# One VectorE product over three joined PSUM banks in place of three, in a linear-attention and mixture-of-experts layer

## The chip, the cores and the metric

The kernel runs on one core of one Trainium2 chip. The metric is the device time of one execution in microseconds (us). Before the change it is 228.59 us, the median of three runs (228.45 to 231.94).

## What is computed

One layer over T = 2048 tokens of width D = 128: linear attention with 16 heads of 8 channels, a layer norm, a mixture of eight experts of which each token uses two, and a second layer norm. The attention is the part that matters here:

```
q = elu(x @ Wq.T) + 1;  k = elu(x @ Wk.T) + 1;  v = x @ Wv.T        # 16 heads of 8
kv        = einsum('blhd,blhe->blhde', k, v)
kv_cumsum = cumsum(kv, axis=1);  k_cumsum = cumsum(k, axis=1)
out = einsum('blhd,blhde->blhe', q, kv_cumsum)
out = out / clip(einsum('blhd,blhd->blh', q, k_cumsum), 1e-06)
x = layernorm(x + out @ Wo.T)
```

After it come the router (softmax over 8 experts, the best two), the experts `gelu(x @ g0) * (x @ g1) @ w`, their weighted sum, and the second layer norm.

## The kernel before

The tokens are cut into 16 chunks of 128 (one token a partition), in four groups of GROUP = 4 chunks. For chunk n the attention goes through these pieces:

- `project` (PE, L566, matmul at L570) gives q, k and v in bank 0. ACT's `inputs` (L778) writes exp, relu and v; `features` (DVE, L983, instruction at L989) makes qk = the two feature maps. v1 holds v with a one behind each head's eight values, so a head has HE = 9 columns and the normalizer comes out as a ninth.
- `outer` (POOL, L475, instruction at L482) forms all products k times v: kv, 128 x 1152 (KV = 16 heads x 9 x 8), once phi_done says that qk is there. It also waits until the matmuls of the chunk four before have read its buffer.
- `prefix` (PE, L573) transposes q (L578) and then multiplies kv by a triangle of ones: the prefix sums within the chunk. The 1152 columns are split by heads into 432, 432 and 288, each in a bank of its own (banks 2, 3, 4, `pre_ps`), with one semaphore step (pre_done) each (L583). Each fp32 matmul shows as two records. Each of the three waits only for VectorE's use of the same bank for the chunk before (pre_used, L581).
- `attend` (DVE, L1002) multiplies each bank by q into prod as its matmul comes in (L1013, three instructions), sums prod over 8 channels into num (L1020), prepares the masked state of the next chunk (`mask_state`, L1000), adds num to what the running state gives (L1029), calls `features` for the chunk three on, takes denominator and reciprocal (L1034, L1037), and writes o (L1041).
- `state` (PE, L586) adds the chunk to the running state (L590) and multiplies the masked state by q (L594, bank 6). `turn_o` (L597, matmul at L601) and `put_out` (L603, L607 and L610) turn o and multiply it by Wo, adding x; ACT copies y out (L807).

Engines run in steps (`groups`, L330): in step m of group g, VectorE attends to chunk m - 1, and PE first does `project` for chunk m + 2, then `prefix` for chunk m - 1, `turn_o` of chunk m - 2, `state` of chunk m - 1 and `put_out` of chunk m - 2 (in steps with route 2, prefix comes first, and four transposes of z, L615, and the logits, L622, stand in between). PE can thus do the prefix of chunk n as soon as it has passed the state and the output of the step before; `turn_o` behind it waits for o of chunk n - 1.

From the second group on, four steps (route 0 to 3) also carry the norm and the routing of the group before, in small instructions that `attend` calls through `between(i)`, i = 0 to 8, after its own instructions: `between(0)`, `between(1)` and `between(2)` stand behind the three products. Route 0: negm at i = 1 (L1081), which ACT's four squares (L817) wait for, then vare at i = 4 (L1088), which POOL's power (L487) waits for, then shift at i = 8 (L1093). POOL's next `outer` stands behind that power. Route 1: nothing in `attend`; ACT normalises to zs, takes inputs, squares zs (L839) and copies zT (L844). Route 2 (`choose`): zsqe at i = 1 (L1104), POOL's second power (L491), the logit at i = 3 and the choice of the best two up to i = 8. Route 3 (`weigh_and_place`): esum and einv at i = 0, prob and gw at i = 1, ren and the copy of the ranks at i = 2 (L1145), then slots up to i = 8 (L1177). In these chains each small instruction waits through `Steps` (dve_steps) for the one before, except where `last` allows more. The last group has its routing done in part behind the last chunk.

POOL then scatters the rows of the last groups to DRAM (L500), a table of tiles is made, and 39 tiles of rows go through the experts (L724 to L753, L1279 to L1294, L537); a last stage adds, normalises and stores.

Of the kernel before, what the change touches and what calls it, by code (L numbers as in the profile page):

```python
# [13 lines left out]
P = 128  # L14
# [3 lines left out]
GROUP = 4  # L18
# [6 lines left out]
H, HD = 16, 8  # L25
HE = HD + 1
KV = H * HE * HD
HEADS = [(0, 6), (6, 12), (12, 16)]
E, K, HID = 8, 2, 256
HB = HID // P  # L30
REGION = T + P
# [43 lines left out]
def build(nc, xT, x, wqkv, wo, rw, rscale, pes, gate_w, lin_w, consts, out):  # L75
# [4 lines left out]
    with ExitStack() as ctx:  # L80
        def sb(name, shape, dt=F32):
            return ctx.enter_context(nc.sbuf_tensor(name, shape, dt))

        def bank(name, shape):
            return ctx.enter_context(nc.psum_tensor(name, shape, F32))

        def sem(name):
            return ctx.enter_context(nc.semaphore(name))
# [3 lines left out]
        def const(name):  # L92
            a, b = CONST[name]
            return C[:, a:b]
# [20 lines left out]
        kv = sb("kv", [P, GROUP, KV])  # L115
        prod = sb("prod", [P, KV])
# [75 lines left out]
        frs = sb("frs", [P, CHUNKS])  # L192
        fshift = sb("fshift", [P, CHUNKS])

        B = [bank(f"bank{i}", [P, 512]) for i in range(8)]

        qkv_ps = B[0]
        pre_ps = B[2:5]
        state_ps = B[5][:, 0:H * HE]
        turn_ps = B[1]  # L200
        qT_ps, oT_ps = B[1][:, 0:P], B[1][:, P:2 * P]
        inter_ps, rank_ps = B[6][:, 0:H * HE], B[6][:, 256:256 + 2 * GROUP * E]
        y_ps, lg_ps = B[7][:, 0:D], B[7][:, 256:256 + GROUP * E]
# [21 lines left out]
        pre_done = sem("pre_done")  # L225
        pre_used = sem("pre_used")
# [8 lines left out]
        summed = sem("summed")  # L235
# [90 lines left out]
        def exists(g, m):  # L326

            return not isinstance(g, int) or 0 <= GROUP * g + m < CHUNKS
# [20 lines left out]
        def after(eng, signal, count):  # L349

            if not (isinstance(count, int) and count <= 0):
                eng.wait_ge(signal, count)
# [112 lines left out]
        def _(pool):  # L465
# [9 lines left out]
            def outer(g, m):  # L475

                n, s = GROUP * g + m, m % GROUP
                pool.wait_ge(phi_done, n + 1)
                after(pool, pre_done, 3 * (n - GROUP + 1))
                a = v1[:, s, :].rearrange("p (h e) -> p h e", e=HE).unsqueeze(3).to_broadcast([P, H, HE, HD])  # L480
                b = qk[:, s, D:2 * D].rearrange("p (h d) -> p h d", d=HD).unsqueeze(2).to_broadcast([P, H, HE, HD])
                pool.tensor_tensor(kv[:, s, :].rearrange("p (h e d) -> p h e d", e=HE, d=HD), a, b,  # L482
                                   ALU.mult).then_inc(kv_done, 1)
# [21 lines left out]
            def step(g, m, route):  # L505
                if route == 0:
                    if g >= 2:
                        scatter(g - 2, (0,))
                    norm_pow(g - 1)
                if route == 2:  # L510
                    rms_pow(g - 1)
                if exists(g, m + 2):
                    outer(g, m + 2)
                if route == 0 and g >= 2:
                    scatter(g - 2, (1,))
                if route == 2 and g >= 2:
                    scatter(g - 2, (2, 3))
# [47 lines left out]
        def _(pe):  # L565
# [7 lines left out]
            def prefix(g, m):  # L573

                n, s = GROUP * g + m, m % GROUP
                pe.wait_ge(phi_done, n + 1)
                after(pe, oT_done, n - 1)
                pe.transpose(qT_ps, qk[:, s, 0:D], const("ident")).then_inc(qTp_done, 1)  # L578
                pe.wait_ge(kv_done, n + 1)
                for b, (h0, h1) in enumerate(HEADS):  # L580
                    after(pe, pre_used, 3 * (n - 1) + b + 1 if not isinstance(g, int) or n else 0)  # L581
                    c0, c1 = h0 * HE * HD, h1 * HE * HD
                    pe.matmul(pre_ps[b][:, 0:c1 - c0], const("tri"), kv[:, s, c0:c1], start=True, stop=True)\  # L583
                      .then_inc(pre_done, 1)

            def state(g, m):  # L586

# [73 lines left out]
            def step(g, m, route):  # L661
                if route == 2:
                    if exists(g, m - 1):
                        prefix(g, m - 1)
                    if exists(g, m + 2):
                        project(g, m + 2)
                    pe.wait_ge(qT_done, GROUP * g + m if exists(g, m - 1) else CHUNKS)
                    turn_z(g - 1)
                    if exists(g, m - 1):
                        state(g, m - 1)  # L670
                    pe.wait_ge(y_used, GROUP * g + m - 2 if exists(g, m - 3) else CHUNKS)
                    logits(g - 1)
                    if exists(g, m - 2):
                        turn_o(g, m - 2)
                        pe.wait_ge(lgs_done, g)
                        put_out(g, m - 2)
                    return
# [88 lines left out]
            for g in PE_PAIRS:  # L766
                c = slice(PAIR * g, PAIR * g + PAIR)
                pe.matmul(sum_ps[g], const("ident"), zall[:, c, :].rearrange("p c d -> p (c d)"),
                          start=True, stop=False)
# [198 lines left out]
        def _(ve):  # L968
# [11 lines left out]
            def heads(t, n=H):  # L980
                return t.rearrange("p (h e) -> p h e", e=HE)

            def features(g, m):  # L983

                n, s = GROUP * g + m, m % GROUP
                ve.wait_ge(act_in, 3 * (n + 1))
                after(ve, state_done, n - GROUP + 1)
                after(ve, kv_done, n - GROUP + 1)
                ve.scalar_tensor_tensor(out=qk[:, s, :], in0=eqk[:, m % 2, :], scalar=1.0, in1=rqk[:, m % 2, :],  # L989
                                        op0=ALU.min, op1=ALU.add).then_inc(phi_done, 1)  # L990

            def mask_state(g, m):

                n = GROUP * g + m
                if isinstance(g, int) and n < 1:
                    ve.wait_ge(state_zero, 1)
                else:
                    ve.wait_ge(state_done, n)
                after(ve, inter_done, n - 1)
                ve.tensor_tensor(state_m[:, m % 2, :], state_ps, const("block"), ALU.mult).then_inc(state_used, 1)  # L1000

            def attend(g, m, between):  # L1002


                n, s = GROUP * g + m, m % GROUP
                q = qk[:, s, 0:D].rearrange("p (h d) -> p h d", d=HD)
                for b, (h0, h1) in enumerate(HEADS):
                    ve.wait_ge(pre_done, 3 * n + b + 1)
                    if b == 0:
                        after(ve, summed, n)  # L1010
                    nh = h1 - h0
                    cols = nh * HE * HD
                    ve.tensor_tensor(  # L1013
                        prod[:, h0 * HE * HD:h1 * HE * HD].rearrange("p (h e d) -> p h e d", e=HE, d=HD),
                        pre_ps[b][:, 0:cols].rearrange("p (h e d) -> p h e d", e=HE, d=HD),
                        q[:, h0:h1, :].unsqueeze(2).to_broadcast([P, nh, HE, HD]), ALU.mult).then_inc(pre_used, 1)
                    between(b)
                ve.wait_ge(pre_used, 3 * (n + 1))
                after(ve, inter_used, n)
                ve.tensor_reduce(num[:, :], prod[:, :].rearrange("p (c d) -> p c d", d=HD), AX.X,  # L1020
                                 ALU.add).then_inc(summed, 1)
                between(3)
                if exists(g, m + 1):
                    mask_state(g, m + 1)
                between(4)
                ve.wait_ge(inter_done, n + 1)
                ve.wait_ge(summed, n + 1)
                after(ve, o_done, n)
                ve.tensor_tensor(inter_ps, inter_ps, num[:, :], ALU.add).then_inc(inter_used, 1)  # L1029
                if exists(g, m + 3):  # L1030
                    features(g, m + 3)
                between(5)
                ve.wait_ge(inter_used, n + 1)
                ve.tensor_scalar(den[:, :], heads(inter_ps)[:, :, HD], DEN_MIN, None, ALU.max).then_inc(den_done, 1)  # L1034
                between(6)
                ve.wait_ge(den_done, n + 1)
                ve.reciprocal(rden[:, :], den[:, :]).then_inc(rden_done, 1)  # L1037
                between(7)
                ve.wait_ge(rden_done, n + 1)
                after(ve, oTp_done, n - 1)  # L1040
                ve.tensor_tensor(o[:, m % 2, :].rearrange("p (h d) -> p h d", d=HD), heads(inter_ps)[:, :, 0:HD],  # L1041
                                 rden[:, :].unsqueeze(2).to_broadcast([P, H, HD]), ALU.mult).then_inc(o_done, 1)
                between(8)
# [209 lines left out]
            a, b = CONST["tile"]  # L1253
# [94 lines left out]
            for j in range(PAIR):  # L1348
                i = PAIR * V_PAIR + j
# [55 lines left out]
```

## Time and profile before

| | us |
|---|---|
| median of three runs | 228.59 (228.45 to 231.94) |
| the profiled execution | 230.38 |
| span of its profile | 228.5 |
| TensorE / VectorE busy | 158.9 / 160.9 |
| ScalarE / GpSimd busy | 101.1 / 124.3 |

All start times below are from the start of the span. The span has three parts: attention with routing to about 107 us, the scatters and the table to about 137 us, then the experts and the last norm. A row's second number is how long an instruction was busy: its records overlap the next one's, so the distance between two starts is what an instruction costs its engine. In a row with x3 it is the length of the three together.

### The profile page before, as it was taken

What the parts mean: (1) busy time and instruction counts of PE and PEld (TensorE: products, weight loads), DVE (VectorE), ACT (ScalarE), POOL (GpSimd) and SP (SyncE); (2) the same over time, 40 slices, a digit from 0 to 9 for tenths busy, and PEclk for the clock granted to TensorE, in tenths of its full rate; (3) what the DMA queues carried; (4) which work ended last, traced back from release to release, by engine and by line L of the source; (5) the groups of instructions that cost most, each with busy time, mean ns of one, the idle gap of its engine ahead of it and who ended that gap; (6) DMA issues with size and microseconds to landing.
All of it is one profiled execution on the core that took longest, in us unless ns stands there. A gap on an engine that the chain in (4) does not pass through costs nothing.

```text
span 228.5 us, 3949 instructions
## 1 busy us (share of the span) xinstructions
PE 158.9 (70%) x768; PEld 114.4 (50%) x769; DVE 160.9 (70%) x535; ACT 101.1 (44%) x359; POOL 124.3 (54%) x114
## 2 busy tenths in 40 slices
PE   2889989576785787675440006999999999971650
PEld 0446655353553545354330004878788888850430
DVE  0489999999989999999769911556655666621760
ACT  3315566472444723476540001556556666620270
POOL 5554643553348576447477750256566566661660
PEclk9999999999799977998555555899999999998575
DMA  5619600020000101010112533022323333215832
GB/s 158 211 27 313 269 17 0 0 80 11 1 23 12 58 12 35 26 71 25 67 51 73 149 94 93 14 79 81 80 82 97 83 82 92 71 46 134 269 96 65
DMA packets 19198, 18.54 MB, mean 81 GB/s; under 512 B 2944, under 2 KB 16256, under 8 KB 19056
## 3 DMA queue, kind: packets, MB, share of 16 engines
q1 hardware_dynamic: 16880, 13.69, 20.2%
q0 software_dynamic: 2304, 4.69, 6.2%
q8 instruction: 4, 0.07, 0.1%
q14 instruction: 10, 0.08, 0.1%
HBM read 10.60 MB, written 6.73 MB: 76 GB/s over the span
## 4 chain that ended last, share of the span: by engine, by line
PE 26%; issue 22%; DVE 18%; POOL 13%; DMA 8%; ACT 7%; DVEq 1%; SPq 1%; POOLq 1%; ACTq 0%
POOL zbuf L500 6%; POOL both L537 6%; DVE prod L1013 5%; PE bank L744 4%; PE bank L583 3%; DVE num L1020 3%; PE bank L570 3%; PE bank L733 3%; DMA both<-yout,zin 2%; PE bank L734 2%; PE bank L735 2%; DMA pl<-both 2%; DMA zin<-zbuf 2%; PE bank L773 2%; PE bank L752 2%
## 5 line engine op out<-in xcount | busy, mean ns | idle before, releaser
L537 POOL DMA_INDIRECT both<-yout,zin x39 | 37.3, 958 | 33.0 <-issue 16.6
L482 POOL TENSOR_TENSOR kv<-v,qk 128x1152 f32<-128x1152 f32 x16 | 34.8, 2174 | 30.6 <-DVE qk L989 30.6
L500 POOL DMA_INDIRECT zbuf<-rows,slot x32 | 32.6, 1018 | 13.7 <-issue 7.7
L583 PE MATMUL bank<-kv,C 128*128 128x432 f32 (+1 forms) x96 | 37.8, 533 | 2.5 <-DVE prod L1013 2.3
L583 PEld LDWEIGHTS bank<-kv,C 128*128 128x128 f32 x96 | 19.0, 212 | 18.8 <-issue 14.2
L1013 DVE TENSOR_TENSOR prod<-bank,qk 128x432 f32<-128x432 f32 (+1 forms) x48 | 24.8, 549 | 1.2 <-DVE slot L1177 0.5
L744 PE MATMUL bank<-w_l,actT 128*128 x156 | 24.7, 281 | 1.1 <-ACT actT L953 1.1
L724 PE MATMUL bank<-C,zin 128*128 128x128 f32 x39 | 11.4, 292 | 19.7 <-DMA zin<-zbuf 19.7
L744 PEld LDWEIGHTS bank<-w_l,actT 128*128 128x128 f32 x156 | 20.5, 190 | 8.9 <-issue 8.8
L1294 DVE COPY yout<-bank 128x128 f32<-128x128 f32 x39 | 11.4, 291 | 19.2 <-PE bank L744 19.2
L1020 DVE TENSOR_REDUCE num<-prod 128x144 f32<-128x1152 f32 x16 | 21.6, 1352 | 0.5
L948 ACT ACTIVATE gelu<-bank 128x256 f32<-128x256 f32 x39 | 14.9, 383 | 13.7 <-PE bank L735 13.7
L570 PE MATMUL bank<-w_qkv,xTs 128*128 128x384 f32 x32 | 17.1, 624 | 5.5 <-DMA xTs<-in_xT 3.5
L953 ACT COPY actT<-bank 128x256 f32<-128x256 f32 x39 | 14.5, 373 | 12.7 <-PE bank L752 12.7
L1279 DVE TENSOR_TENSOR zin_lo<-bank,zin_hi 128x128 fp32r<-128x128 f32 x39 | 11.4, 291 | 12.5 <-ACT zin_hi L943 8.6
L1287 DVE SCALAR_TENSOR_TENSOR act<-gelu,zin,bank 128x256 f32<-128x256 f32 x39 | 18.4, 472 | 2.3 <-ACT gelu L948 2.3
L733 PE MATMUL bank<-w_hi,zin_hi 128*128 x39 | 19.7, 505 | 0.0
L943 ACT CAST zin_hi<-bank 128x128 fp32r<-128x128 f32 x39 | 10.6, 271 | 20.0 <-PE bank L724 20.0
L724 PEld LDWEIGHTS bank<-C,zin 128*128 128x128 f32 x39 | 5.8, 148 | 20.5 <-DMA zin<-zbuf 20.4
L734 PE MATMUL bank<-w_lo,zin_hi 128*128 x39 | 16.0, 409 | 0.0
L735 PE MATMUL bank<-w_hi,zin_lo 128*128 x39 | 15.9, 408 | 0.0
L752 PE MATMUL bank<-C,act 128*128 128x128 f32 x78 | 15.1, 276 | 0.0
(152 smaller groups left out, 339.0 us busy)
## 6 DMA issues: line engine op xcount, KB each, us to landing
zin<-zbuf SPq DMA_DIRECT2D x39, 65.0 KB, 1.8
w_g<-in_gate_w SPq DMA_DIRECT2D x4, 512.0 KB, 5.9
pl<-both SPq DMA_DIRECT2D x8, 256.0 KB, 4.8
xTs<-in_xT SPq DMA_DIRECT2D x16, 64.0 KB, 2.2
w_l<-in_lin_w SPq DMA_DIRECT2D x1, 1024.0 KB, 9.1
zall<-zs SPq DMA_DIRECT2D x4, 256.0 KB, 2.4
out<-pl SPq DMA_DIRECT2D x8, 128.0 KB, 1.8
both<-yout,zin POOLq DMA_INDIRECT x39, 2.2
```

Of the source, the lines that this page charges most:

```text
L482: pool.tensor_tensor(kv[:, s, :].rearrange("p (h e d) -> p h e d", e=HE, d=HD), a, b, ALU.mult).then_inc(kv_done, 1)
L500: pool.indirect_dma_start(zbuf, bass.IndirectOffsetOnAxis(ap=slot_of(g)[:, c:c + 1].bitcast(U32), axis=0), rows_of(g)[:, j, r, :], None)\
L537: pool.indirect_dma_start(both, bass.IndirectOffsetOnAxis(ap=zin[:, b, D + 1:D + 2].bitcast(U32), axis=0), yout[:, b, :], None).then_inc(p ...
L570: pe.matmul(qkv_ps[:, 0:3 * D], xTs[:, m % GROUP, :], w_qkv[:, :], start=True, stop=True)\
L583: pe.matmul(pre_ps[b][:, 0:c1 - c0], const("tri"), kv[:, s, c0:c1], start=True, stop=True)\
L733: pe.matmul(g, zin_hi[:, b % 2, :], hi, start=True, stop=False)
L734: pe.matmul(g, zin_hi[:, b % 2, :], lo, start=False, stop=False)
L735: pe.matmul(g, zin_lo[:, b % 2, :], hi, start=False, stop=True).then_inc(gate_done, 1)
L744: mm = pe.matmul(yout_ps[b % 2][:, 0:D], actT[:, b % 2, h, :], w_l[:, bass.ds(e * (HB * D) + h * D, D)], start=(h == 0), stop=(h == HB - 1))
L752: mm = pe.transpose(actT_ps[b % 2][:, h * P:(h + 1) * P], act[:, b % 2, h * P:(h + 1) * P], const("ident"))
L1013: ve.tensor_tensor(prod[:, h0 * HE * HD:h1 * HE * HD].rearrange("p (h e d) -> p h e d", e=HE, d=HD), pre_ps[b][:, 0:cols].rearrange("p (h ...
L1020: ve.tensor_reduce(num[:, :], prod[:, :].rearrange("p (c d) -> p c d", d=HD), AX.X, ALU.add).then_inc(summed, 1)
```

## The change

The three banks become one PSUM tensor of 1536 columns. The 1152 prefix sums lie in it without gaps, so that the matmuls are cut at bank ends (512, 512, 128 columns) and no more between heads. PE waits once for the whole use of the chunk before and signals once after the third matmul; VectorE waits once, multiplies all 1152 columns in one instruction, and calls `between(0)`, `between(1)` and `between(2)` after it. The counts of pre_done and pre_used go by one a chunk. Banks 0, 1, 5, 6 and 7, and what the expert stage uses, stay where they were.

```diff
-HEADS = [(0, 6), (6, 12), (12, 16)]
+BANK = 512
+KV_PARTS = [(a, min(a + BANK, KV)) for a in range(0, KV, BANK)]
...
-        B = [bank(f"bank{i}", [P, 512]) for i in range(8)]
+        b01 = [bank(f"bank{i}", [P, BANK]) for i in range(2)]
+        b234 = bank("bank234", [P, 3 * BANK])
+        B = b01 + [b234[:, i * BANK:(i + 1) * BANK] for i in range(3)] + [bank(f"bank{i}", [P, BANK]) for i in range(5, 8)]
...
-        pre_ps = B[2:5]
+        pre_ps = b234[:, 0:KV]
...
-                after(pool, pre_done, 3 * (n - GROUP + 1))
+                after(pool, pre_done, n - GROUP + 1)
...
-                for b, (h0, h1) in enumerate(HEADS):
-                    after(pe, pre_used, 3 * (n - 1) + b + 1 if not isinstance(g, int) or n else 0)
-                    c0, c1 = h0 * HE * HD, h1 * HE * HD
-                    pe.matmul(pre_ps[b][:, 0:c1 - c0], const("tri"), kv[:, s, c0:c1], start=True, stop=True)\
-                      .then_inc(pre_done, 1)
+                after(pe, pre_used, n)
+                for c0, c1 in KV_PARTS:
+                    mm = pe.matmul(pre_ps[:, c0:c1], const("tri"), kv[:, s, c0:c1], start=True, stop=True)
+                mm.then_inc(pre_done, 1)
...
-                for b, (h0, h1) in enumerate(HEADS):
-                    ve.wait_ge(pre_done, 3 * n + b + 1)
-                    if b == 0:
-                        after(ve, summed, n)
-                    nh = h1 - h0
-                    cols = nh * HE * HD
-                    ve.tensor_tensor(
-                        prod[:, h0 * HE * HD:h1 * HE * HD].rearrange("p (h e d) -> p h e d", e=HE, d=HD),
-                        pre_ps[b][:, 0:cols].rearrange("p (h e d) -> p h e d", e=HE, d=HD),
-                        q[:, h0:h1, :].unsqueeze(2).to_broadcast([P, nh, HE, HD]), ALU.mult).then_inc(pre_used, 1)
+                ve.wait_ge(pre_done, n + 1)
+                after(ve, summed, n)
+                ve.tensor_tensor(
+                    prod[:, :].rearrange("p (h e d) -> p h e d", e=HE, d=HD),
+                    pre_ps.rearrange("p (h e d) -> p h e d", e=HE, d=HD),
+                    q.unsqueeze(2).to_broadcast([P, H, HE, HD]), ALU.mult).then_inc(pre_used, 1)
+                for b in range(3):
                     between(b)
-                ve.wait_ge(pre_used, 3 * (n + 1))
+                ve.wait_ge(pre_used, n + 1)
```

## Rows read from the trace of the kernel before

**Rows 1.** The page's first part: busy time by engine.
```profile
PE 158.9 (70%) x768; PEld 114.4 (50%) x769; DVE 160.9 (70%) x535; ACT 101.1 (44%) x359; POOL 124.3 (54%) x114
```

**Rows 2.** Busy time in one stretch of 20 us; PEclk is the granted clock.
```profile
40.00:60.00 20.00, 12.58 (x63) 8.61 (x63) 19.50 (x55) 8.64 (x37) 8.55 (x5) 0.98 0.09 27
```

**Rows 3.** Groups by line and form, 12 to 132 us: the products.
```profile
L1013 DVE TENSOR_TENSOR prod<-bank,qk 128x432 f32<-128x432 f32 x32 | 18.2, 600 | 0.9 <-DVE slot L1177 0.5
L1013 DVE TENSOR_TENSOR prod<-bank,qk 128x288 f32<-128x288 f32 x16 | 7.2, 447 | 0.4 <-PE bank L583 0.4
```

**Rows 4.** Timeline of VectorE, chunk 3: start us, busy us, instruction [idle before].
```profile
27.20 1.48 DVE L1013 TENSOR_TENSOR prod<-bank,qk 128x432 f32<-128x432 f32 x3
27.71 0.60 DVE L1013 TENSOR_TENSOR prod<-bank,qk 128x432 f32<-128x432 f32 x1
28.71 1.35 DVE L1020 TENSOR_REDUCE num<-prod 128x144 f32<-128x1152 f32 x1
29.98 0.30 DVE L1000 TENSOR_TENSOR state_m<-bank,C 128x144 f32<-128x144 f32 x1
```

**Rows 5.** Timeline of PE and VectorE, chunk 1 at the start.
```profile
17.57 2.10 PE L583 MATMUL bank<-kv,C 128*128 128x432 f32 x6
...
18.50 1.70 DVE L1013 TENSOR_TENSOR prod<-bank,qk 128x432 f32<-128x432 f32 x3
20.24 1.35 DVE L1020 TENSOR_REDUCE num<-prod 128x144 f32<-128x1152 f32 x1
```

**Rows 6.** Timeline of VectorE and POOL, a step with route 0 (chunk 9).
```profile
65.02 1.12 DVE L1013 TENSOR_TENSOR prod<-bank,qk 128x432 f32<-128x432 f32 x2 [0.48 <-DVE slot L1177]
66.06 0.16 DVE L1081 TENSOR_SCALAR negm<-ysum 128x4 f32<-128x4 f32 x1
...
68.52 0.17 DVE L1088 TENSOR_SCALAR vare<-ssq 128x4 f32<-128x4 f32 x1 [0.34 <-ACT junk L817]
...
69.80 2.16 POOL L482 TENSOR_TENSOR kv<-v,qk 128x1152 f32<-128x1152 f32 x1
69.89 2.10 DVE L1093 TENSOR_TENSOR shift<-negm,rstd 128x4 f32<-128x4 f32 x1
```

**Rows 7.** Timeline of VectorE, POOL and ACT, a step with route 2 (chunk 7).
```profile
47.09 2.18 POOL L482 TENSOR_TENSOR kv<-v,qk 128x1152 f32<-128x1152 f32 x1 [3.65 <-DVE qk L989]
47.63 1.11 DVE L1013 TENSOR_TENSOR prod<-bank,qk 128x432 f32<-128x432 f32 x2
48.66 0.64 DVE L1104 TENSOR_SCALAR zsqe<-zsq 128x4 f32<-128x4 f32 x1
...
49.69 1.35 DVE L1020 TENSOR_REDUCE num<-prod 128x144 f32<-128x1152 f32 x1
...
50.24 0.18 ACT L856 COPY lgs<-bank 128x32 f32<-128x32 f32 x1 [0.48 <-PE bank L622]
...
50.96 0.18 DVE L1053 TENSOR_TENSOR r_logit<-lgs,rrms 128x32 f32<-128x32 f32 x1
```

**Rows 8.** Timeline of VectorE, a step with route 3 (chunk 8).
```profile
56.16 0.61 DVE L1013 TENSOR_TENSOR prod<-bank,qk 128x432 f32<-128x432 f32 x1
...
56.69 0.18 DVE L1062 TENSOR_REDUCE r_esum<-r_elog 128x4 f32<-128x32 f32 x1
56.90 0.18 DVE L1066 RECIPROCAL r_einv<-r_esum 128x4 f32<-128x4 f32 x1
...
58.21 0.18 DVE L1062 TENSOR_REDUCE r_ren<-r_gw 128x4 f32<-128x32 f32 x1
...
58.44 1.34 DVE L1020 TENSOR_REDUCE num<-prod 128x144 f32<-128x1152 f32 x1
```

**Rows 9.** Timeline of PE: the prefix matmuls of chunks 7 and 12.
```profile
44.05 2.20 PE L583 MATMUL bank<-kv,C 128*128 128x432 f32 x6 [1.15 <-DVE prod L1013]
...
81.04 3.14 PE L583 MATMUL bank<-kv,C 128*128 128x432 f32 x6
```

**Rows 10.** Timeline of POOL: a scatter behind the attention.
```profile
119.46 0.96 POOL L500 DMA_INDIRECT zbuf<-rows,slot  x1 [0.30 <-ACT rows L864]
```

## The prediction

> **What bounds the kernel now.** I read the page first. No engine is busy all the time: VectorE has 160.9 of 228.5 us, PE 158.9 [rows 1]. So I went on to stretches. [...] Behind 107 us the change touches nothing. Then I read the timelines of all engines step by step, because "busy" deceives here: shift, an instruction on four columns, is busy for 2.10 us [rows 6]. It starts when POOL's kv has just begun and ends when kv ends (69.80 + 2.16 = 71.96). VectorE is held there, not working. So the question is, step by step, whether the bound is VectorE's own work, such a hold, or a chain through ACT.
>
> **One product for three.** The groups give 600 ns for 432 columns and 447 for 288 [rows 3]: 153 ns for 144 columns, 1.06 ns a column, and 141 ns besides. 1152 columns then take 1.22 + 0.14 = 1.36 us. The sum over 1152 columns has the same 1.35 us [rows 4]. Now num starts 28.71 - 27.20 = 1.51 us after the first product; the new one would let it start after 1.36 and 0.03 of semaphore, 1.39. The gain is 0.12 us a chunk, not twice the 0.14 us that each removed instruction has of its own, since neighbours overlap: the second product starts 0.51 after the first, whose record is 0.60 long [rows 4]. An instruction that needs nothing of the product starts 1.27 after it, as state_m does behind num (29.98 - 28.71) [rows 4].
>
> [...]
>
> **Product and matmuls no longer overlap.** VectorE must now wait for the third matmul, and PE for the whole product. Both ends: where the other engine is ready anyway the cost is 0; where it isn't, up to the length of the one not hidden, 2.1 us for the six records of PE at the full clock. I take it place by place.
> - Start. Chunk 1's matmuls end at 17.57 + 2.10 = 19.67. The three products now begin at 18.50 and num at 20.24 [rows 5]. Afterwards the product starts at 19.73 and num at 21.12: a loss of 0.88. Chunk 0 is late in the same way, but PE is the one that is waited for there, and it doesn't wait for VectorE.
> - Chunks 2 to 4. PE's prefix of the next chunk lies beside VectorE's num and what follows it. A chunk takes some 4.3 us; a serial pair of 1.39 and 2.1 leaves 0.8. I take 0 for the wait and the gain of 0.12 three times: +0.88 becomes +0.52. The lowest would be +0.3 (the late start partly absorbed), the highest +1.3.
> - Later steps with a PE wait: chunk 7's matmuls start at 44.05 when chunk 6's first product (43.4) has been read [rows 9]. They would start at 44.8, or 45.2 with what the start has lost, and end at 47.4; VectorE wants them at 47.63 + 0.4 = 48.0 [rows 7]. 0.6 us of cover remains. Queued behind them on PE are project, the transposes of z (for ACT's zT) and state; ACT is busy with squares till then. Cost 0. If the matmuls took 3.14 us as in chunk 12 [rows 9], the product would be 0.35 late.
> - POOL's wait on pre_done has the end of chunk n - 4; nothing hangs on it.
>
> **The small instructions, moved behind the product.**
> - Route 0 (chunks 5, 9, 13). negm starts 66.06 - 65.02 = 1.04 after the product [rows 6], afterwards 1.27: 0.23 later. On negm hangs a chain that VectorE waits for: ACT's squares, vare (VectorE idle 0.34 before it), POOL's power, POOL's kv, and shift, held until kv ends [rows 6]. So what the product gives is not gained, and 0.23 is lost. In chunk 5 negm is held by POOL's kv till after the product in both versions: 0 there, 0.23 in each of chunks 9 and 13.
> - Route 1 (chunks 6, 10, 14): no small instructions; gain 0.12.
> - Route 2 (chunks 7, 11, 15). zsqe is held till kv ends (47.09 + 2.18 = 49.27) and the third product, some 0.45, comes after it; num is at 49.69 [rows 7]. With all columns multiplied under kv, num can stand directly behind zsqe: 0.45 earlier than now relative to kv. But r_logit also needs lgs from ACT (50.24 + 0.18 = 50.42, against 50.96) [rows 7], and that comes through ACT from shift without a pause. So r_logit moves forward at most 0.5 against shift's own shift.
> - Route 3 (chunks 8, 12). Each step of the chain esum, einv, prob, gw, ren waits for the one before, 0.21 apart (56.90 - 56.69) [rows 8]; now two products cover two of these waits. Afterwards: 1.27 to esum, 4 x 0.21 to ren, 0.23 from ren to num (58.44 - 58.21), 2.34 in all against 58.44 - 56.16 = 2.28 [rows 8]. Loss 0.06. The lower end would be a gain of 0.14 (waits free), the upper a loss of 0.3.
>
> **The sum**, as VectorE's delay against before: +0.52 after chunk 4; +0.52 (chunk 5); +0.40 (6); at chunk 7 r_logit follows ACT, +0.52 - 0.51 = 0; +0.06 (8); +0.29 (9); in chunks 10 and 11 VectorE gains more than ACT lets through, so 0.29 - 0.5 = -0.2; -0.15 (12); +0.08 (13); -0.04 (14); -0.16 (15, where no kv stands in the way and only the product's 0.12 is gained). From there it goes one to one through the last routing and the scatters of POOL, the first of which wait for ACT's rows [rows 10], to the expert stage. The profiled execution took 230.38 us (span 228.5); it would take 230.2. It lies 1.8 above the median of 228.59, so the change is applied to that: 228.4. Two per cent, 4.6 us, is about what a measurement of this kernel can tell from no change; this is far inside.
>
> **Rivals.**
> 1. VectorE's own work is the bound everywhere (0.98 busy speaks for it, the holds against it). Then 16 x 0.12 = 1.9 us, and 3 x 0.35 more in route 2, less the 0.9 of the start: 2.1 faster, 226.5. Chance 0.18.
> 2. An instruction costs its whole fixed part, so that each removed one gives it back: 32 x 0.14 = 4.5 us, 224.1. The start distances [rows 4] speak against it. Chance 0.03.
> 3. The matmuls come onto the path. [...] Three times 1.4, with 0.2 of gain kept: +3.3 with the transposes and zT behind them partly beside it, 231.9. [...] Chance 0.18. [...]
> 4. The joined read is slower than three, or the joined tensor adds a stall; with 0.15 ns a column more it is 16 x 0.17 = 2.8 us, 231.2. No row has a read over a bank's end. Chance 0.05.
>
> My forecast has 0.56. Its own range is 227.4 to 229.6; with rivals 1 and 3 taken in, 226.4 to 231.4. Faster by over 2% (below 224.0) 0.02, slower by over 2% (above 233.2) 0.03, within 0.95.
>
> **What would show it.** L1013 with 16 instructions of 1.36 us and num 1.39 after each start in steps without routing; in route 2 zsqe held as before and num directly behind it; negm 1.27 after the product; route 3 with 2.3 from product to num; PE's matmuls 2.1 to 2.2 long and over before VectorE is through with o, in all chunks but 0 and 1. The forecast is wrong if VectorE is seen idle before L1013 in later chunks (rival 3), if the product is longer than 1.45 (rival 4), or if chunk 15's o comes more than 1 us earlier than now (rivals 1, 2).

## The result, and the profile after

The changed kernel takes 234.72 us (median of four runs, 232.63 to 235.37) against 228.84 for the kernel before: 5.9 us more, a ratio of 1.024 with an interval of 1.017 to 1.031. Beside other kernels on a second chip it was 232.82 against 228.32, ratio 1.0245 (1.019 to 1.030). The ratios leave out runs that lie far above the fastest of the same kernel (one of the second chip's six took 263.51), so they differ from the quotients of the medians, most for e12 below. The change is slower beyond doubt; whether by more than 2% the intervals leave open. I had forecast 228.4 with a range up to 231.4; the truth lies outside, on the side of my third rival. The profiled execution took 234.94 us, its span is 233.1 (before: 230.38 and 228.5).

First the busy times of the page, and the same 20 us stretch as in [rows 2] (columns: length, then busy time and count of PE, PEld, DVE, ACT, POOL, then the granted clock, DMA share, GB/s).

```profile
PE 161.1 (69%) x768; PEld 114.7 (49%) x769; DVE 158.3 (68%) x503; ACT 101.6 (44%) x359; POOL 124.5 (53%) x114
```

```profile
40.00:60.00 20.00, 13.58 (x54) 8.52 (x54) 16.74 (x42) 8.37 (x34) 7.88 (x5) 0.83 0.08 26
```

VectorE lost its 32 instructions and 2.6 us of busy time (holds by POOL's kv, such as the 2.10 us of shift in [rows 6], are counted in it), and the kernel is slower: in this stretch VectorE was busy for 19.50 us and is now for 16.74, and PE's clock went from 0.98 to 0.83. So VectorE waits, and the first suspect is PE. The product's own size is as forecast; the groups by form (12 to 132 us) show the product and the matmuls, first the matmuls of the kernel before:

```profile
L583 PE MATMUL bank<-kv,C 128*128 128x432 f32 x63 | 28.8, 583 | 2.5 <-DVE prod L1013 2.3
```

```profile
L585 PE MATMUL bank<-kv,C 128*128 128x512 f32 x63 | 34.5, 675 | 5.8 <-DVE prod L1011 5.8
L1011 DVE TENSOR_TENSOR prod<-bank,qk 128x1152 f32<-128x1152 f32 x16 | 21.7, 1354 | 4.9 <-PE bank L585 4.0 <-DVE slot L1176 0.5 <-issue 0.2
```

The product waits 4.0 us for the matmuls, 0.4 before [rows 3], and the matmuls 5.8 for the product, 2.3 before. Where, the timelines tell. PE's prefix matmuls of chunks 7, 11 and 12, the first and the third to be held against [rows 9]:

```profile
43.95 4.18 PE L585 MATMUL bank<-kv,C 128*128 128x512 f32 x6 [1.99 <-DVE prod L1011]
...
75.06 4.18 PE L585 MATMUL bank<-kv,C 128*128 128x512 f32 x6 [2.00 <-DVE prod L1011]
...
84.40 2.10 PE L585 MATMUL bank<-kv,C 128*128 128x512 f32 x6
```

Six records of chunk 7 took 2.20 us before, at a granted clock of 1.00 (44.05 to 46.25), and take 4.18 now, at 0.50 (43.95 to 48.13), twice the 2.10 of chunk 12 at the upper level (1.00, 84.40 to 86.50). Ahead of them PE idles 1.99 us where it idled 1.15. The chain of waits from the product of chunk 6 on shows what it does to the whole kernel:

```profile
42.46 1.36 DVE prod L1011
43.82 0.14 issue
43.95 4.18 PE bank L585 x6
48.13 1.28 PE bank L573 x2
49.41 0.63 PE bank L617 x4
50.04 0.02 issue
50.06 0.59 ACT zT L846
50.65 0.14 issue
50.79 1.04 PE bank L624 x8
51.83 0.02 issue
51.85 0.20 ACT lgs L858
```

From 43.95 to 51.83 PE is on the path almost alone: the slow matmuls, project (1.28 to the next start at a granted 0.50, in place of 0.65 at the upper level, 51.11 to 51.76 before), the transposes of z, then the logits. Two waits end last on VectorE, its product and, after it, r_logit (chunk 7, timeline of VectorE, POOL and ACT, against [rows 7]):

```profile
46.03 2.17 POOL L485 TENSOR_TENSOR kv<-v,qk 128x1152 f32<-128x1152 f32 x1 [3.52 <-DVE qk L991]
...
48.17 1.36 DVE L1011 TENSOR_TENSOR prod<-bank,qk 128x1152 f32<-128x1152 f32 x1 [1.51 <-PE bank L585]
49.44 0.16 DVE L1103 TENSOR_SCALAR zsqe<-zsq 128x4 f32<-128x4 f32 x1
49.56 1.35 DVE L1019 TENSOR_REDUCE num<-prod 128x144 f32<-128x1152 f32 x1
...
51.85 0.19 ACT L858 COPY lgs<-bank 128x32 f32<-128x32 f32 x1 [0.48 <-PE bank L624]
...
52.17 0.19 DVE L1052 TENSOR_TENSOR r_logit<-lgs,rrms 128x32 f32<-128x32 f32 x1 [1.26 <-ACT lgs L858]
```

The product is held for 1.51 us and r_logit for another 1.26. zsqe, busy 0.64 before while POOL's kv held it, is busy 0.16: kv is over when it comes (46.03 + 2.17 = 48.20).

The start of each first product, read off both timelines, gives the place of the loss in one table:

| chunk (route) | before | after | difference |
|---|---|---|---|
| 3 | 27.20 | 26.59 | -0.61 |
| 5 (0) | 36.24 | 35.31 | -0.93 |
| 6 (1) | 43.40 | 42.46 | -0.94 |
| 7 (2) | 47.63 | 48.17 | +0.54 |
| its r_logit | 50.96 | 52.17 | +1.21 |
| 8 (3) | 56.16 | 57.33 | +1.17 |
| 9 (0) | 65.02 | 66.45 | +1.43 |
| 10 (1) | 71.91 | 73.57 | +1.66 |
| 11 (2) | 76.14 | 79.27 | +3.13 |
| its r_logit | 79.48 | 83.09 | +3.61 |
| 13 (0) | 93.09 | 96.84 | +3.75 |
| 14 (1) | 97.86 | 101.83 | +3.97 |

From chunk 6 to the end the difference moves from -0.94 to the 4.6 us between the spans, by 5.5. Two jumps, 2.15 us at chunk 7 and 1.95 at chunk 11, are 4.1 of that; 0.8 comes in small steps between and behind them. The scatter that waits for ACT's rows [rows 10] is 3.98 later, and the last 0.6 comes behind it, for which no row here gives the cause:

```profile
123.44 0.96 POOL L503 DMA_INDIRECT zbuf<-rows,slot  x1 [0.30 <-ACT rows L866]
```

The small terms can be checked on the same timelines. Chunks 1 and 3, for [rows 5] and [rows 4]:

```profile
16.19 2.10 PE L585 MATMUL bank<-kv,C 128*128 128x512 f32 x6
...
18.33 1.36 DVE L1011 TENSOR_TENSOR prod<-bank,qk 128x1152 f32<-128x1152 f32 x1 [0.73 <-PE bank L585]
...
26.59 1.36 DVE L1011 TENSOR_TENSOR prod<-bank,qk 128x1152 f32<-128x1152 f32 x1
27.98 1.35 DVE L1019 TENSOR_REDUCE num<-prod 128x144 f32<-128x1152 f32 x1
```

Route 0, chunk 9, for [rows 6], and route 3, chunk 8, for [rows 8]:

```profile
57.33 1.35 DVE L1011 TENSOR_TENSOR prod<-bank,qk 128x1152 f32<-128x1152 f32 x1
...
59.72 1.34 DVE L1019 TENSOR_REDUCE num<-prod 128x144 f32<-128x1152 f32 x1
...
66.45 1.36 DVE L1011 TENSOR_TENSOR prod<-bank,qk 128x1152 f32<-128x1152 f32 x1 [0.47 <-DVE slot L1176]
67.72 0.16 DVE L1080 TENSOR_SCALAR negm<-ysum 128x4 f32<-128x4 f32 x1
...
70.18 0.17 DVE L1087 TENSOR_SCALAR vare<-ssq 128x4 f32<-128x4 f32 x1 [0.77 <-ACT junk L819]
```

num starts 1.39 us after the product, negm 1.27 after it, and 2.39 lie between product and num in route 3.

### The profile page after: what moved, and what is told of

Same layout as the page of the kernel before. It is cut to its first block, busy times and chain, and to the rows that moved or that the text cites. A ratio compares the mean times of both kernels' runs of the same rounds, so it can differ in the third digit from the quotient of the medians.

```text
span 233.1 us, 3875 instructions
## 1 busy us (share of the span) xinstructions
PE 161.1 (69%) x768; PEld 114.7 (49%) x769; DVE 158.3 (68%) x503; ACT 101.6 (44%) x359; POOL 124.5 (53%) x114
## 4 chain that ended last, share of the span: by engine, by line
PE 27%; issue 24%; POOL 16%; DVE 12%; DMA 11%; ACT 4%; SPq 1%; DVEq 1%; POOLq 1%; ACTq 0%
POOL zbuf L503 8%; PE bank L585 6%; POOL both L540 6%; DMA both<-yout,zin 3%; PE bank L573 3%; DMA zin<-zbuf 3%; PE bank L746 3%; DVE prod L1011 2%; PE bank L735 2%; DMA pl<-both 2%; PE bank L736 2%; DMA xTs<-in_xT 2%; PE bank L737 2%; PE bank L775 1%; DVE num L1019 1%
## 5 line engine op out<-in xcount | busy, mean ns | idle before, releaser
L585 PE MATMUL bank<-kv,C 128*128 128x512 f32 (+1 forms) x96 | 39.3, 551 | 5.8 <-DVE prod L1011 5.8
L1011 DVE TENSOR_TENSOR prod<-bank,qk 128x1152 f32<-128x1152 f32 x16 | 21.7, 1354 | 4.9 <-PE bank L585 4.0
```

Source lines behind the costliest of these rows:

```text
L585: mm = pe.matmul(pre_ps[:, c0:c1], const("tri"), kv[:, s, c0:c1], start=True, stop=True)
L1011: ve.tensor_tensor(prod[:, :].rearrange("p (h e d) -> p h e d", e=HE, d=HD), pre_ps.rearrange("p (h e d) -> p h e d", e=HE, d=HD), q.unsqu ...
```

## The experiments

Theory A: PE must wait for the whole product, idles longer before the prefix of chunks 7 and 11, and its clock falls. Theory B: what costs is that product and matmuls no longer overlap, at any clock. Times are medians. The four sets (e1 to e4; e5 to e8; e9 to e12; e13 to e16) ran each on a chip of its own, with the kernel before beside them (229.11, 228.32, 229.49 and 228.87 us); between sets the ratios are what can be compared.

**e1, PE's wait alone.**

```diff
+                after(pe, pre_used, 3 * n)
                 for b, (h0, h1) in enumerate(HEADS):
-                    after(pe, pre_used, 3 * (n - 1) + b + 1 if not isinstance(g, int) or n else 0)
```

> The kernel before, with one edit: PE waits for all three products of the chunk before ahead of its first prefix matmul, as in the change; three banks, three products and three signals stay. [...] Theory B (what costs is that product and matmuls no longer overlap, whatever the clock): at most 0.5 us slower, since the product here still begins behind the first matmul.

Measured: 233.37 against 229.11, ratio 1.012 (1.008 to 1.017). The matmuls of chunks 7 and 11:

```profile
44.12 3.81 PE L583 MATMUL bank<-kv,C 128*128 128x432 f32 x6 [2.02 <-DVE prod L1013]
...
73.64 3.19 PE L583 MATMUL bank<-kv,C 128*128 128x432 f32 x6 [2.03 <-DVE prod L1013]
```

As theory A has it, by the medians (+4.3): idle 2.0, the clock low for most of both (granted 0.57 and 0.67). By the ratio it is 2.8 us, just under the 3 to 4.5 that A expected, and about half of the change's 5.5. Theory B's 0.5 is passed either way.

**e2, VectorE's wait alone.**

```diff
-                    ve.wait_ge(pre_done, 3 * n + b + 1)
                     if b == 0:
+                        ve.wait_ge(pre_done, 3 * n + 3)
```

> The kernel before, with one edit: VectorE waits for the third matmul of the chunk ahead of its first product; PE may still refill each bank as it comes free. Theory A: PE's idle time and clock stay as before, 0 to 1 us slower (only the start of the attention pays). Theory B: nearly all of the loss of the change, 3 to 5 us slower.

Measured: 230.83, ratio 1.008 (1.004 to 1.013), 1.7 us by the medians and 1.9 by the ratio: more than A's upper end, well short of B. The start accounts for 1.1: chunk 5's first product begins at 36.52, against 35.46 in e4, which differs from the kernel before only behind chunk 5, both with first matmuls of 3.5 us. And one of its two matmul groups was slow (3.67 us, granted clock 0.59), though PE idled only 1.14:

```profile
44.32 3.67 PE L583 MATMUL bank<-kv,C 128*128 128x432 f32 x6 [1.14 <-DVE prod L1013]
...
73.02 2.20 PE L583 MATMUL bank<-kv,C 128*128 128x432 f32 x6 [1.16 <-DVE prod L1013]
```

**e3, the changed kernel with PE kept busy; e4, the kernel before with the same.** In route 2 steps, before the wait for the product; in route 1 the state's own matmul leaves its signal to the last of the six.

```diff
                 pe.transpose(qT_ps, qk[:, s, 0:D], const("ident")).then_inc(qTp_done, 1)
+                for _ in range(warm):
+                    mm = pe.matmul(state_ps, zero[:, 0:P], zero[:, :], start=False, stop=False,
+                                   skip_group_check=True)
+                if warm:
+                    mm.then_inc(state_done, 1)
...
```

> The changed kernel, with six small matmuls of zeros times zeros added to the running state (they add nothing) ahead of the prefix matmuls of chunks 7, 11 and 15, where PE waits for the whole product. [...] Theory B: no faster than the changed kernel, 234 or more, since PE has more to do and overlaps as little.

> The kernel before with the same six small matmuls at the same place, as a control. Theory A: the clock was full there already, so within 1 us of before, up to 0.5 us slower where they hold back the prefix. If instead it gets faster by 2 us or more, the small matmuls help somewhere else, and the gain of the run with the changed kernel says less about chunks 7 and 11.

Measured: e3 228.94, ratio to before 1.000 (0.997 to 1.003), so the whole loss of the change is gone (theory A expected 229 to 231); e4 229.82, ratio 1.003 (1.000 to 1.006), the control. In e3:

```profile
41.98 1.64 PE L584 MATMUL bank<-zero 128*128 128x144 f32 x12
44.13 2.18 PE L591 MATMUL bank<-kv,C 128*128 128x512 f32 x6 [0.52 <-DVE prod L1019]
...
73.14 2.18 PE L591 MATMUL bank<-kv,C 128*128 128x512 f32 x6 [0.53 <-DVE prod L1019]
```

Both groups ran at a granted clock of 1.00. Product and matmuls overlap as little as in the changed kernel, and more work made it some 4 to 6 us faster. Theory B falls as the main cause; what is left of it is the start and the 1.9 us at most that e2 shows.

**e8, the changed kernel once more; e5, with negm ahead of the product.**

```diff
+                first()
                 ve.wait_ge(pre_done, n + 1)
...
-                    if route is not None:
+                    if route is not None and (route, i) != (0, 1):
...
-                    attend(g, m - 1, between)
+                    attend(g, m - 1, between, (lambda: parts[0](g - 1, 1)) if route == 0 else (lambda: None))
```

> The changed kernel as it is, beside the others on the same chip: both theories expect 233 to 235.5, 4 to 6 us over the kernel before, with the prefix matmuls of chunks 7 and 11 at about 4.2 us.

> The changed kernel with negm (route 0) ahead of the product in place of behind it. My step on route 0 says that negm starts the chain that VectorE waits for (squares, vare, power, kv, shift), and that the change put it from 1.04 to 1.27 us behind the product's start. If that is right: negm comes 1.2 to 1.3 us earlier, VectorE's idle time before vare (0.62 to 0.81 us three times) goes, and the time falls by 1.5 to 2.5 us against the changed kernel run beside it; the prefix matmuls of chunks 7 and 11 stay at 4.2 us. If route 0 is not a bound, no change.

Measured: e8 232.82, with 3.68 and 3.78 us for the matmuls of chunks 7 and 11; e5 230.71 (ratio 1.010, 1.006 to 1.014), so 2.1 us for moving one instruction on four columns. Chunk 9 in e5: negm stands before the product, and vare has no idle time before it (0.77 in the changed kernel).

```profile
66.64 0.17 DVE L1081 TENSOR_SCALAR negm<-ysum 128x4 f32<-128x4 f32 x1 [0.38 <-DVE slot L1177]
66.86 1.36 DVE L1012 TENSOR_TENSOR prod<-bank,qk 128x1152 f32<-128x1152 f32 x1
...
69.73 0.16 DVE L1088 TENSOR_SCALAR vare<-ssq 128x4 f32<-128x4 f32 x1
```

The clock stayed low for most of its chunk 7 (3.67 us, granted 0.59) and partly in 11 (2.92, 0.72). My reading of route 0 holds.

**e6, six zero matmuls and negm first; e7, six more in route 3**, between the ranks and the wait for rank_used.

> The changed kernel with both: six zero matmuls ahead of the prefix of chunks 7, 11 and 15, and negm ahead of the product. If the two causes are separate, their gains add: 226.5 to 228, 1 to 2 us under the run with the zero matmuls alone (228.94) and 1 to 2.5 under the kernel before. If negm only moves the wait to somewhere else, 229.

> The run before this one, with six more zero matmuls in the steps of route 3, where PE waits for VectorE to copy the ranks and its clock then falls (prefix of chunk 9 and 13: 3.4 to 3.7 us in the run with zero matmuls, with VectorE idle 0.92 before one of their products). If an idle PE is what lowers the clock there too: those prefixes take 2.1 us and the time falls by 0.5 to 1.5 us more, to 225.5 to 227. If something else sets the clock: no change.

Measured: e6 226.68, ratio to before 0.996 (0.993 to 0.999): the gains add. e7 226.74 (0.996, 0.992 to 1.000), nothing more. Its prefixes of chunks 9 and 13 did take 2.10, but chunk 14's took 3.87 at a granted 0.56, with VectorE idle 1.05 before its product: a miss, the low clock only came at another place.

**e9, the kernel before with negm first; e12, the kernel before with both waits.** e9 is e5's edit in `attend` of the kernel before, `first()` ahead of its loop; e12 is e1 and e2 together.

> The kernel before with negm ahead of its first product: how much of the best version so far (226.68) comes from the joined product at all. In the changed kernel this edit gave 2.1 us. If the joined product brings nothing beside it, this run is as fast, 226 to 227.5; if the joined product brings its 0.12 us a chunk, this run is 1 to 2 us slower than that, 227.5 to 228.5. PE's matmuls of chunks 7 and 11 should stay at 2.2 us.

> The kernel before with both waits of the change (PE for the whole use, VectorE for the third matmul), but still three products in three banks: what is left to the change is the joined instruction and the place of the small instructions. By my steps the joined product gains 0.12 us a chunk, some 1.5 to 2 us in all, less two times 0.23 for negm, so this run should be 1 to 2 us slower than the changed kernel (232.8 beside the last runs), 233.5 to 235.5. If it is as slow as the changed kernel or faster, the joined product itself gains nothing.

Measured: e9 227.62, ratio to before 0.994 (0.990 to 0.999), which is as good as e6 (0.996): without any joined product. Its 227.62 lies at the seam of my two ranges, so it is the ratios that say this. Its chunk 7 kept the clock (granted 1.00), chunk 11 did not (0.59), after the same idle time of 1.2:

```profile
44.13 2.20 PE L583 MATMUL bank<-kv,C 128*128 128x432 f32 x6 [1.17 <-DVE prod L1014]
...
72.25 3.71 PE L583 MATMUL bank<-kv,C 128*128 128x432 f32 x6 [1.18 <-DVE prod L1014]
```

e12 took 234.52 with before at 229.49, +5.0, and e8 232.82 with before at 228.32, +4.5. The ratios, 1.014 (1.006 to 1.022) and 1.0245 (1.019 to 1.030), point the other way. So the gain of the joined instruction, 1 to 2 us by my expectation, can't be read from this pair. What it does say: both waits without the joined product cost 5.0 us by the medians and 3.2 by the ratio, most of what the change costs, and the matmuls of chunks 7 and 11 take 4.21 us there, at a granted 0.50.

**e10 and e11, one and three zero matmuls in place of six.**

> The changed kernel with one zero matmul (0.25 us at the full clock) in place of six: same order, same semaphores (the signal for the running state given late too), hardly more work for PE. If the gain of the six came from PE being busy: PE is idle some 1.75 us instead of 0.5, and the time stays at 232 to 234.5. If it came from the order or the later signal: 228.5 to 229.5 as with six.

> The changed kernel with three zero matmuls: PE idle about 1.25 us ahead of the prefix of chunks 7 and 11, near the 1.15 of the kernel before. If the idle time decides, the clock mostly holds and the time is near the one with six, 228.5 to 230.5; if any gap of a microsecond lowers it, 232 or more.

Measured: e10 229.13 (ratio 1.001, 0.998 to 1.005), e11 229.67 (1.002, 0.999 to 1.004). Three matmuls did what I expected of them. One does all that six do, against my expectation. In e10 it leaves PE idle for 1.74 us ahead of chunk 7's matmuls, which ran at a granted 1.00:

```profile
42.29 0.41 PE L584 MATMUL bank<-zero 128*128 128x144 f32 x2
44.44 2.18 PE L591 MATMUL bank<-kv,C 128*128 128x512 f32 x6 [1.74 <-DVE prod L1019]
```

Its two records are busy 0.41 us, but overlap what follows. What it costs PE is 0.25: six of them closed the gap from 1.99 to 0.52 (e3), and in e13, below, the matmul behind one starts 0.25 after it, at a granted 1.00:

```profile
41.15 0.41 PE L593 MATMUL bank<-zero 128*128 128x144 f32 x2
41.40 0.41 PE L594 MATMUL bank<-v,qk 128*128 128x144 f32 x2
```

Either 1.75 us of idle time is short enough, or the order did it.

**e13 and e14, one zero matmul in two places, signals untouched.** In e13 it stands right ahead of the state's own matmul in route 1 steps; in e14 ahead of `turn_o`, in another gap of PE:

```diff
+                if route == 1:
+                    pe.wait_ge(state_used, GROUP * g + m)
+                    pe.matmul(state_ps, zero[:, 0:P], zero[:, :], start=False, stop=False, skip_group_check=True)
                 if exists(g, m - 2):
                     turn_o(g, m - 2)
```

> The changed kernel with one zero matmul right ahead of the state's own in the steps of route 1; no signal is moved. It pushes PE's work to within about 1.75 us of the prefix matmuls of chunks 7, 11 and 15. If the gap ahead of them decides the clock: 228.5 to 230, their matmuls 2.2 us. If the one-zero run gained by its later signal: as the changed kernel, 232 to 235.

> The changed kernel with the same zero matmul ahead of turning o in the steps of route 1, where PE also idles (1.4 us) for VectorE. The gap ahead of the prefix stays 2.0 us. If that gap decides: as the changed kernel, 232 to 235. If PE's work over a longer stretch decides: faster, 228.5 to 231.

Measured: e13 229.05, ratio 1.001 (0.997 to 1.005); e14 233.24, ratio 1.021 (1.016 to 1.026). In e13:

```profile
44.35 2.18 PE L585 MATMUL bank<-kv,C 128*128 128x512 f32 x6 [1.75 <-DVE prod L1013]
...
72.90 2.18 PE L585 MATMUL bank<-kv,C 128*128 128x512 f32 x6 [1.76 <-DVE prod L1013]
```

and in e14:

```profile
43.85 4.18 PE L585 MATMUL bank<-kv,C 128*128 128x512 f32 x6 [1.99 <-DVE prod L1014]
...
74.91 2.18 PE L585 MATMUL bank<-kv,C 128*128 128x512 f32 x6 [2.00 <-DVE prod L1014]
```

The same work, once behind which the gap is 1.75 and once with the gap left at 2.0: 4.2 us apart, with chunk 7's matmuls at a granted 1.00 in e13 and at 0.50 in e14. The later signal and the total work are excluded; it matters that the work stands next to that gap. The gap alone is not a switch, though: e14's chunk 11 kept the clock (1.00) behind 2.00 us in the profiled execution, which was the fastest of its six (231.51).

**e15 and e16, both edits on either kernel.**

> The kernel before with negm ahead of its first product and one zero matmul as in the one-zero run. Three separate products. The clock in chunks 7 and 11 stays at the upper level in more executions than in the run with negm alone (there one of two fell): 226 to 227.5.

> The changed kernel with negm ahead of the product and one zero matmul. If the joined product gains its 0.12 us a chunk once the clock and negm are out of the way, it is 0.5 to 2 us faster than the run beside it; if its start (VectorE waits for the third matmul) eats that, they are equal within 0.5. 225.5 to 227.

Measured: e15 227.80, ratio 0.994 (0.990 to 0.998), just above its range and no better than e9, with 2.20 us in chunks 7 and 11; e16 228.94, ratio 1.006 (1.002 to 1.011). Beside each other the version with three products is 1.1 us faster. e16 missed its expectation, in its time and in that it is the slower one; its chunks 7 and 11 ran at the upper level (2.17 and 2.18, granted 1.00), but chunks 9 and 13 took 3.38 and 3.60 (0.62 and 0.58), and chunk 9's product waited 0.32 for them. With six zero matmuls (e6) chunk 9 took 2.10.

## Why the prediction was wrong, by its steps

- **The product.** Right: 1.36 us forecast, 1.354 measured; num 1.39 behind it; product 1.27 to the next that needs nothing. Neighbours overlap, as read: two products of 0.60 us start 0.51 apart [rows 4].
- **The start.** Right in size. Chunk 1's product waits (0.73), and e2 shows 1.06 us for VectorE's wait, of which four joined products give 0.5 back. e8's chunk 5 starts at 36.04 against 35.44 in e1, of which 0.17 is its longer first matmuls (3.69 against 3.52): 0.43, where I had 0.52. That the profiled execution was 0.93 ahead at chunk 5 is not the change: the first matmuls took 2.94 in place of 4.04. That PE's clock rose sooner there is my estimate from these two lengths; the granted clock that the profile gives is 1.00 over both.
- **Later steps with a PE wait, "Cost 0".** This is the step that failed. I had the new start of chunk 7's matmuls about right (0.75 us later against chunk 6's product; it was 0.84) and their end at 2.1 us behind it. I had also seen that PE would idle 0.75 longer, but left the length at the upper level, because the trace showed that after 1.15 us of idle time. At 2.0 us it isn't so: 4.18 in place of 2.1, at a granted 0.50. My cover of 0.6 was gone, and 1.51 of wait took its place.
- **What stands behind on PE.** I wrote that project, the transposes and the state were covered by ACT's squares. With the clock down they were not: zT waited 2.43 us for PE's transposes, where before it followed the squares without a pause, and r_logit waited 1.26 more. ACT's zT, before and after:

```profile
48.46 0.56 ACT L844 COPY zT<-bank 128x512 f32<-128x512 f32 x1
```

```profile
50.06 0.59 ACT L846 COPY zT<-bank 128x512 f32<-128x512 f32 x1 [2.43 <-PE bank L617]
```

That is why rival 3 was under-priced too. Its 1.4 us a place was my estimate for matmuls of 4.2 us (twice 2.10) that end at 49.4, against the 48.0 at which VectorE wants them, and it counted three places. No run shows a loss of 1.4 us a place; the changed kernel lost 2.15 and 1.95, and in two places only. In chunk 15 no kv holds shift, so PE waited only 0.24 and the matmuls took 2.17.
- **Route 0.** Right: negm 1.27 behind the product, 0 in chunk 5 (-0.93 to -0.94), +0.23 from chunk 9 to 10, +0.22 from 13 to 14. e5 confirms it from the other side.
- **Route 2.** The 0.45 us that multiplying under POOL's kv would save never came, since the product began behind kv. Where the clock was held it came in part: in e13 the product starts under kv (46.97, kv until 48.61), num stands at 48.55, and r_logit is 3.05 us behind the product, against 3.33 before.
- **Route 3.** 2.39 from product to num where I had 2.34, against 2.28 before. The whole step cost 0.26 in chunk 8 and 0.13 in chunk 12, more than my 0.06, within my upper 0.3.
- **The chance.** Rival 3 had 0.18. Its mechanism (PE idles longer ahead of the matmuls in route 1 steps, 1.99 us in place of 1.15, and its clock falls, 1.00 to 0.50), its place and its direction are what happened; against it I had the full clock behind 1.15 us of idle time, and weighed that too heavily, with two instances at 1.15 us and none at 2.0. PE's wait alone (e1) costs half of the change's loss by the ratios and three quarters by the medians; VectorE's (e2) costs less.
- **The rest of the sum.** My forecast is a ratio of 0.999 to the kernel before. With the clock held in chunks 7 and 11 the changed kernel has 1.000, 1.001 and 1.001 (e3, e10, e13), so the other terms together came out. The joined product thus pays for its start and for the later negm, and no more; beside negm put first it even lost (e16 against e15), and of these 1.1 us only 0.32 is seen, the wait of chunk 9's product.

What stays open: idle time alone does not explain all. In the profiles with a gap of 2.0 us ahead of chunks 7 and 11 (the changed kernel twice, e1, e5, e12, e14) 11 of 12 groups were slow; with the joined product and gaps of 0.5 to 1.8 (e3, e6, e7, e10, e11, e13, e16) none of 14; but in the three-bank kernels with 1.15 (before, e2, e9) 2 of 6, and with 0.9 and one zero matmul (e15) none of 2. What else PE had done before wasn't varied separately.

## What to carry to other kernels

An idle engine costs nothing only if its speed doesn't hang on it: before a wait of PE is made longer, price the work behind it at PE's lower clock too (granted 0.50 here, 4.18 us in place of 2.10), not only at the level that the trace shows after the shorter wait, and follow that price to everything queued behind. Then look at the small instruction that is moved with a large one; negm was worth 2.1 us by its place alone, of which the change itself had cost some 0.5. Of all versions here the cheapest good one leaves the three products alone and only puts negm first (227.62, ratio 0.994); e6 is as fast (0.996) but needs work that computes nothing. Both gains are well under 1%.

## What the runs showed of the hardware

PE's granted clock hung on a quarter of a microsecond next to one gap: matmuls behind 1.99 us of idle time ran at a granted 0.50 (4.18 us for six records, e14), behind 1.75 us at 1.00 (2.18 us, e13), and a matmul of zeros with zeros was enough as work (e10, e13). It is a tendency and no threshold: behind 2.0 us 11 of 12 groups were slow, behind 1.15 us 2 of 6. The two profiled executions of the changed kernel differ in it: chunk 7's records took 4.18 us in one (granted 0.50) and 3.68 in the other (0.59), both behind 1.99 us of idle time. In e2, e9 and e14 two places with equal gaps came out differently within one execution (3.67 and 2.20, 2.20 and 3.71, 4.18 and 2.18 us); what decides there no run here shows.

One VectorE product over three joined PSUM banks took 1.354 us for 1152 columns. The line through 432 and 288 columns in one bank [rows 3] gives 1.36, so reading across bank ends cost nothing that these traces can show.
